# Runtime offsets loaded eight at a time, three cuts moved between engines, and the router product turned round, in a fused cross-attention and mixture-of-experts kernel

## What is computed

```python
x = x + tanh(g_xattn) * xattn(layernorm(x), ctx, mask, W, b)   # scores from relu projections, softmax over 77 keys
h = layernorm(x)
logits = h @ w_router                     # 8 experts, top 2, softmax over the two
moe = sum over the 2 chosen e of score * (silu(h @ fc1[e][:, :256]) * (h @ fc1[e][:, 256:])) @ fc2[e]
shared = (silu(h @ gate_w) * (h @ up_w)) @ down_w              # hidden width 512
x = x + tanh(g_ffn) * (moe + shared)
```

## Time and profile before

| | us |
|---|---|
| median of 3 runs | 240.33 |
| the profiled execution | 240.49 |
| its span in the trace | 238.8 |
| TensorE matmul busy | 216.5 (91%) |
| VectorE busy | 168.6 (71%) |
| ScalarE busy | 134.2 (56%) |
| GpSimd busy | 124.4 (52%) |

### The profile page before, as it was taken

How to read it: one execution, slowest core, us unless ns; L and a number is a source line. 1 busy time by engine, 2 the same in 40 slices (tenths; PEclk the granted TensorE clock), 3 DMA queues, 4 the chain that set the end, 5 groups by cost and what they waited for, 6 DMA issues and landing times.

```text
span 238.8 us, 5190 instructions
## 1 busy us (share of the span) xinstructions
PE 216.5 (91%) x1347; PEld 187.2 (78%) x1347; DVE 168.6 (71%) x513; ACT 134.2 (56%) x332; POOL 124.4 (52%) x178
## 2 busy tenths in 40 slices
PE   7988999999899999889727999999999999999982
PEld 7778899978687888668616788888888888887761
DVE  1978897797569799996912866666575666654893
ACT  2555888798769734445212465656566565655320
POOL 1698997554867877888400043434434343443600
PEclk9999999999999999999985999999999999999999
DMA  4999930000131225322003348475565646319787
GB/s 155 287 403 405 406 148 0 0 3 23 45 117 45 91 72 204 137 85 97 2 22 60 69 111 124 111 129 111 124 122 113 135 100 133 60 38 299 236 283 281
DMA packets 39347, 32.13 MB, mean 135 GB/s; under 512 B 29254, under 2 KB 30539, under 8 KB 39320
## 3 DMA queue, kind: packets, MB, share of 16 engines
q1 hardware_dynamic: 35312, 22.31, 34.0%
q0 software_dynamic: 3408, 8.53, 10.9%
q10 hardware_dynamic: 600, 0.97, 1.2%
HBM read 14.84 MB, written 12.75 MB: 116 GB/s over the span
## 4 chain that ended last, share of the span: by engine, by line
PE 59%; SPq 12%; issue 8%; DVE 8%; POOL 4%; DMA 3%; ACT 3%; DVEq 0%; POOLq 0%; ACTq 0%
PE bank L1028 41%; SPq L286 7%; PE bank L1291 3%; PE bank L1062 3%; PE bank L1074 2%; SPq L282 2%; DMA xt<-rows 2%; DMA acc<-in_x 2%; PE bank L1102 1%; PE bank L1164 1%; DVE act_lo L664 1%; SPq L281 1%; DVE acc L740 1%; PE bank L1112 1%; SPq L292 1%
## 5 line engine op out<-in xcount | busy, mean ns | idle before, releaser
L445 POOL DMA_INDIRECT parts<-y_out,dst x39 | 38.8, 995 | 70.9 <-DVE dst L957 46.1
L403 POOL DMA_INDIRECT rows<-hwords,slot x32 | 34.0, 1062 | 12.3 <-issue 10.7
L1028 PE MATMUL bank<-ew_hi,m_xt_hi 128*128 x78 | 31.6, 406 | 6.3 <-DVE m_xt_lo L664 6.3
L963 DVE TENSOR_TENSOR act<-act,bank 128x256 f32<-128x256 f32 x39 | 16.4, 421 | 29.5 <-issue 19.1
L615 ACT ACTIVATE act<-bank 128x256 f32<-128x256 f32 x39 | 15.0, 384 | 36.6 <-PE bank L1028 36.6
L1028 PE MATMUL bank<-ew_lo,m_xt_hi 128*128 x78 | 31.3, 401 | 0.0
L1028 PE MATMUL bank<-ew_hi,m_xt_lo 128*128 x78 | 31.3, 401 | 0.0
L1028 PE MATMUL bank<-ew_hi,act_hi 128*128 x78 | 25.2, 323 | 0.2 <-issue 0.2
L458 ACT ACTIVATE act_hi<-act 128x512 fp32r<-128x512 f32 x16 | 10.1, 629 | 25.4 <-DVE act L726 9.5
L664 DVE TENSOR_TENSOR m_xt_lo<-xt,m_xt_hi 128x256 fp32r<-128x256 f32 x39 | 16.2, 416 | 8.3 <-ACT m_xt_hi L458 8.3
L1028 PE MATMUL bank<-ew_lo,act_hi 128*128 x78 | 21.9, 280 | 0.0
(11 more groups left out here) (186 smaller groups left out, 644.4 us busy)
## 6 DMA issues: line engine op xcount, KB each, us to landing
ew_raw<-in_chunks SPq DMA_DIRECT2D x12, 512.0 KB, 10.7
low_buf<-parts SPq DMA_DIRECT2D x4, 512.0 KB, 3.6
high_buf<-parts SPq DMA_DIRECT2D x4, 512.0 KB, 4.0
acc<-in_x SPq DMA_DIRECT2D x7, 256.0 KB, 5.4
sw_raw<-in_chunks SPq DMA_DIRECT2D x3, 512.0 KB, 8.3
out<-acc SPq DMA_DIRECT2D x3, 512.0 KB, 3.3
rows<-pad_rows SPq DMA_DIRECT2D x9, 132.0 KB
xt<-rows SPq DMA_TRANSPOSE x39
```

The lines of the kernel that those rows point to most:

```text
L403: pool.indirect_dma_start(out=rows, out_offset=bass.IndirectOffsetOnAxis(ap=slot[:, h, k, i:i + 1], axis=0), in_=hwords[:, HT * h + i, :], ...
L445: pool.indirect_dma_start(out=parts, out_offset=bass.IndirectOffsetOnAxis(ap=dst[:, t:t + 1], axis=0), in_=y_out[:, t % SLOTS, :], in_offs ...
L963: TT(act[:, p, 0:I], act[:, p, 0:I], M_H[p][:, I:2 * I], ALU.mult).then_inc(s["m_prod"], 1)
L1028: ins = pe.matmul(ps, a, b, start=first and i == 0, stop=last and i == total - 1, skip_group_check=not lone)
```

## The change

Four edits.

1. SP reads the 39 offsets with five register loads of up to eight values, and without the bounds check behind each.
2. GpSimd's three `LAST` cuts go to VectorE, whose table gives units 7, 8, 10 and 11 one cut more and unit 12 one less. From unit 8 on, one cut stands ahead of `product_lo` and the rest behind it.
3. The router product is turned round. `wr` is widened to 352 columns a slice, zero but for 16, so that a window of 128 columns puts the 16 logits of group g on partitions 16 (g mod 4) and up. The weights stand still and 256 tokens move: four matmuls a group, four groups summed into the same 256 columns of bank 6. GpSimd clears `wr` at the start.
4. The logits of a half now lie with the experts on the partitions. VectorE copies them out (`cut_logits`), TensorE turns them back with two transposes (`turn_logits`) behind `gate(0)` and behind `gate(3)`, and VectorE reads them. In the last attention step VectorE's `turn_e` now stands ahead of `read_logits` and `first_choice`.

```diff
-LAST = tuple(range(CHUNKS - 3, CHUNKS))
-LATER = {3: 1, 4: 1, 5: 1, 6: 1, 7: 1, 8: 1, 9: 2, 10: 2, 11: 2, 12: 3}
+LATER = {3: 1, 4: 1, 5: 1, 6: 1, 7: 2, 8: 2, 9: 2, 10: 3, 11: 3, 12: 2}
...
-            off = [sp.value_load(t_off[0:1, t:t + 1], min_val=0, max_val=2 * PAD_ROW) for t in range(N_TILES)]
+            off = []
+            for t in range(0, N_TILES, 8):
+                off += nc.values_load_multi_w_load_instructions(
+                    t_off[0:1, t:min(t + 8, N_TILES)], engines=(mybir.EngineType.SP,), min_val=0, max_val=2 * PAD_ROW,
+                    skip_runtime_bounds_check_because="t_off is a row of the table or PAD_ROW, by construction")[1]
...
+            pool.memset(wr[:].bitcast(F32), 0.0).then_inc(s["wr_z"], 1)
...
-            for i in LAST:
-                cut_lo(pool, i)
...
+            def cut_logits(h):
+                after(v, "lg_ps", HG * (h + 1))
+                after(v, "lg_turned", h)
+                v.tensor_copy(lgt[:], bank[6][0:HG * 2 * E, 0:GN]).then_inc(s["lg_cut"], 1)
...
-                cut_later(u)
+                cut_later(u, slice(0, 1))
                 product_lo(u)
+                cut_later(u, slice(1, None))
...
             def router(g):
                 after(pe, "ht_l", g + 1)
+                at_ = g % HG
+                if at_ == 0:
+                    after(pe, "lg_cut", g // HG)
+                w_ = slice(WZ - 2 * E * at_, WZ - 2 * E * at_ + P)
+                for k in range(K):
+                    for x_ in (ht_hi, ht_lo):
+                        ins = pe.matmul(bank[6][:, 0:GN], wr[:, k, w_], x_[:, k, g * GN:(g + 1) * GN],
+                                        start=at_ == 0 and k == 0 and x_ is ht_hi,
+                                        stop=at_ == HG - 1 and k == K - 1 and x_ is ht_lo, skip_group_check=True)
+                ins.then_inc(s["lg_ps"], 1)
+
+            def turn_logits(h):
+                after(pe, "lg_cut", h + 1)
+                after(pe, "lg_read", h)
+                n_ = HG * 2 * E
                 for j in range(GT):
...
+                    ins = pe.transpose(bank[6][:, GN + j * n_:GN + (j + 1) * n_], lgt[:, j * P:(j + 1) * P],
+                                       ident[0:n_, 0:n_])
+                ins.then_inc(s["lg_turned"], 1)
...
             gate(0)
+            turn_logits(0)
             scores(NG - 1)
...
-            gate_up(3)
+            gate(3)
+            turn_logits(1)
+            up(3)
```

More of the change, by code:

```diff
@@ L47 @@
 HT = NT // NH
+HG = NG // NH
+WZ = 2 * E * (HG - 1)
 IN_A = 7
@@ L153, in build @@
         wr_raw = sm[:, 2 + K:].rearrange("p (k e) -> p k e", e=E)
-        wr = sb("wr", [P, K, 2 * E], F32R)
+        wr = sb("wr", [P, K, WZ + P], F32R)
+        lgt = sb("lgt", [HG * 2 * E, GN])
         tg = sb("tg", [P, 2])
@@ L207, in build @@
             xt_ps xt_h xt_l wt_h wt_l y_h y_l xp_ps xp sc_ps sc_in sc_max sc_exp eT_ps eT_h eT_l mt_ps s_inv resid stats2 mean2 pre2 pow2 rstd2 h_ready h_planes
-            hT_ps ht_h ht_l lg_ps lg_read rt picked rank_ps placed wts low_expert w_sign w_tanh fields slots t_expm scattered pads tb tiles_known
+            hT_ps ht_h ht_l wr_z lg_ps lg_cut lg_turned lg_read rt picked rank_ps placed wts low_expert w_sign w_tanh fields slots t_expm scattered pads tb tiles_known
             chunk_h chunk_lp chunk_lv gate_ps up_ps sil prod act_h act_l dn_ps dn_added
@@ L244, in by_pool @@
         def by_pool(i):
-            return i < IN_A or i in MID + LAST
+            return i < IN_A or i in MID
         def chunks_at(slot_):
@@ L469, in _ @@
             a.activation(tg[:], sm[:, 0:2], ACT.Tanh).then_inc(s["tanh_g"], 1)
-            hi(wr[:, :, 0:E], wr_raw, "wr_h")
+            after(a, "wr_z", 1)
+            hi(wr[:, :, WZ:WZ + E], wr_raw, "wr_h")
             a.wait_ge(wt_in, 16)
@@ L778, in then @@
                 v.wait_ge(s[name], n[name])
+            def cut_logits(h):
+                after(v, "lg_ps", HG * (h + 1))
+                after(v, "lg_turned", h)
+                v.tensor_copy(lgt[:], bank[6][0:HG * 2 * E, 0:GN]).then_inc(s["lg_cut"], 1)
             def read_logits(h):
-                after(v, "lg_ps", (NG // NH) * (h + 1))
-                lp = bank[6][:, HT * h * 2 * E:HT * (h + 1) * 2 * E].rearrange("p (t e) -> p t e", e=2 * E)
-                v.tensor_copy(lgx[:], lp).then_inc(s["lg_read"], 1)
+                after(v, "lg_turned", h + 1)
+                lp = bank[6][:, GN:GN + HT * 2 * E].rearrange("p (j g e) -> p g j e", j=GT, g=HG)
+                v.tensor_copy(lgx[:].rearrange("p (g j) e -> p g j e", j=GT), lp).then_inc(s["lg_read"], 1)
             def top(h, k):
@@ L822, in slots, with cut_later @@
                 v.tensor_copy(slot[:, h], slotf[:]).then_inc(s["slots"], 1)
-            def cut_later(u):
-                mine = [i for i in range(IN_A, CHUNKS) if i not in MID + LAST]
+            def cut_later(u, some=slice(None)):
+                mine = [i for i in range(IN_A, CHUNKS) if i not in MID]
                 first = sum(m for w, m in LATER.items() if w < u)
-                for i in mine[first:first + LATER.get(u, 0)]:
+                for i in mine[first:first + LATER.get(u, 0)][some]:
                     cut_lo(v, i)
@@ L884, in _ @@
             product_lo(2)
+            cut_logits(1)
             read_logits(1)
@@ L1107, in router @@
                 after(pe, "ht_l", g + 1)
-                for j in range(GT):
[L1109 to L1116, removed]
+                at_ = g % HG
[12 more added lines that the diff above has]
+                n_ = HG * 2 * E
+                for j in range(GT):
+                    ins = pe.transpose(bank[6][:, GN + j * n_:GN + (j + 1) * n_], lgt[:, j * P:(j + 1) * P],
+                                       ident[0:n_, 0:n_])
+                ins.then_inc(s["lg_turned"], 1)
             def rank_in_tile(h, ps):
@@ L1304, in _ @@
             down(U0 - 2)
-            after(pe, "chunk_lp", IN_A + len(MID + LAST))
-            after(pe, "chunk_lv", CHUNKS - IN_A - len(MID + LAST))
+            after(pe, "chunk_lp", IN_A + len(MID))
+            after(pe, "chunk_lv", CHUNKS - IN_A - len(MID))
             after(pe, "sil", U0)
```

7 lines of the change are left out of this document (4 added, 3 removed).

## The result

Four timed runs of the changed kernel gave 231.25 to 234.17 us, median 233.1; the kernel before had a median of 240.25 beside them (238.93 to 242.0). The ratio is 0.969, with a 95% interval from 0.960 to 0.978: faster. The forecast was 230.6 us with a range of 229.0 to 233.8. Direction and range held; of the 9.9 us that the sum promised, 7.2 came. The median lies outside the forecast's own range, 229.4 to 232, and inside that of rival B, 231.5 to 234, which had a chance of 0.15.

A forecast was written before the change was run, and what follows sets the result against it. SP's 39 offset reads were taken to delay the routed tiles. First load 8.9 us earlier plus 1.0 us from stage 1 makes 9.9 us off 240.49, so 230.6 us, range 229.0 to 233.8.

The forecast's parts named there:

- rival B: TensorE and VectorE arrive at the routed tiles later than the loads, through more stalls; 231.5 to 234 us, chance 0.15.
- the limit of 0.35 us a value: SP's offset loads: only above this price would they outlast their 10.6 us of slack and decide the first load.
- the old step of 0.57 us: SP's time per single offset read before, taken as the price of each wide load: five make about 3 us.
- the replay on the old scale: Stage 2's products and cuts from product 12 on, re-timed with edit 2: `m_up(0)` at 119.2 instead of 126.93 us.
- The stall of unit 8: TensorE's wait in stage 2, expected near 1.8 us after the change.
- I give them 0.6 us: Stage 1, VectorE's first and second choice ahead of the ranks: gain allowed despite an added copy of about 0.35 us.
- I take 1.0 us for stage 1 together: Edit 3's gain where unit 3 starts: 1.0 us earlier, between 0.4 and 3.0 us.
- GpSimd's later scatters ... so move too: Scatters from the cut at 72.17 us, which waits 1.48 us for ScalarE behind `gate(3)`, shift along with stage 1.
- The loads decide: Start of the routed tiles: first transposing load at 113.3 us sets the time; TensorE's path has 1.0 us to spare.
- Rival C: Router's saving reaches the scatters nearly whole, 2.0 to 3.0 us instead of 1.0; about 229 us, chance 0.08.
- D: Wide offset loads priced by value at the old step, so only stage 1's 1.0 us is kept; 239.5 us, chance 0.04.
- E: Wide offset loads cost more per value than the old step; at 0.8 us a value 248 us, chance 0.02.

The follow-up runs named there:

- e_offsets: The kernel before with edit 1 alone (five offset loads of eight, no bounds check); median 233.35 us, ratio 0.982 to before.
- a_no_router: The kernel before with edits 1 and 2, so without the turned router and its VectorE order; median 229.9 us, ratio 0.966 to before.
- k_fill: The changed kernel plus eight unused identity matmuls on TensorE ahead of the last attention step's `turn_e`; median 231.61 us, ratio 0.970 to before.
- l_singles: The changed kernel with 39 single offset loads instead of five of eight, still without bounds check; median 232.26 us, ratio 0.972 to before.
- f2: The changed kernel with GpSimd's cuts 5 and 6 moved between `weight_fields(0)` and the first scatter; median 230.75 us, ratio 0.966 to before.
- e_router: The kernel before with edits 3 and 4 alone (router turned round); median 241.55 us, ratio 1.014 to before.
- after_again: The changed kernel itself, unaltered, run again in a later set; median 231.63 us, ratio 0.963 to before.

## Why the prediction was right, and where its size was off

**Edit 1** was right. Five loads were taken at 3 us and cost 3.6; the limit of 0.35 us a value was not reached (about 0.09). What became late next was named rightly, the scattered rows. e_offsets has its first load at 114.36 us, where 114.3 was forecast. The Trainium skill's floor of about 600 ns for a `tensor_load` (DMA: Bandwidth & Descriptors, section Latency and other measured facts), quoted beside that term, is not borne out: single loads took 0.27 us and wide ones 0.52 to 0.94. Nor did the old step of 0.57 us speak for it, since the load was 0.27 us of that. The measurement decides; the sum did not rest on it.

**Edit 2** was right for TensorE: the idle time before `down(12)` is gone, and the replay on the old scale, `m_up(0)` at 119.2 us, is what a_no_router shows (119.23). The step that failed is that the first load was left at 114.3 us whatever edit 2 does. In a_no_router it came at 112.83, relative to x 1.7 us earlier than in e_offsets: the last scatter 1.2 us earlier, and its landing 0.5 us sooner. Since the loads did not decide in the end, this slip cost nothing. The stall of unit 8 was overrated, 1.40 us where "near 1.8" was forecast, and 1.14 in a_no_router.

**Edit 3** had the wrong sign, and that is where the time went. The failed step reads "I give them 0.6 us", for the choices, and "I take 1.0 us for stage 1 together". The local prices were sound: a router group took 0.55 us (forecast 0.48), steps 5 to 7 took 4.94 to 4.95 us each (forecast 4.9). But the sum took the choices at the length that they had before (they end at 51.85 us) and added a copy, although VectorE's and GpSimd's instructions beside each other had just been used to explain the 4.55 us of the earlier trace rows. The same rule (the Trainium skill, SBUF — State Buffer, section Who interferes with whom: two SBUF inputs on VectorE against a GpSimd instruction that reads SBUF, the later one waits for the whole of the other) bears on the choice, whose comparisons have two SBUF inputs; the rows of 1.19 and 1.21 us agree with it. Without the turned router one operation was hit so, 0.95 us long in a_no_router. The new order hits two, and both stand ahead of the softmax that TensorE waits for. At full clock the router's order and its way to the logits together cost 1.2 to 1.3 us at `m_up(0)` and at the last scatter (k_fill and l_singles against a_no_router), of which f2 gives back 0.7 to 0.9. In six of ten runs some 1.5 us of clock come on top. This is with edits 1 and 2 in; for the router alone e_router leaves it open.

**"GpSimd's later scatters ... so move too"** was the other half of the slip: they did move with stage 1, but to a later time.

**The end.** "The loads decide" with 1.0 us of slack for TensorE did not come out. In the changed kernel ScalarE cut the first two tiles at once behind the activation (no wait for a load), so TensorE's own stream decided, which is rival B, though for another reason than it gave: it expected more stalls in stage 2, and the time went at the end of stage 1. The loads decided in none of the runs with edit 1. Even in l_singles the chain that ended last goes from ScalarE's cut of the last activation over VectorE to `m_up(0)`, not over SP.

Put together from the traces, relative to x, at the start of `down(15)`: edits 1 and 2 gave 9.7 us (216.58 in a_no_router, 226.26 before) where 8.9 was forecast, and the router took 2.3 to 2.5 where it was to give 1.0. The final sums behind that were 0.9 to 1.1 us shorter than before, a gain that the forecast had left out ("nothing in the change touches them or the tail") and that no run explains. So the span gained 8.0 to 8.5 us against 9.9, a sum of one large miss and two smaller ones of the other sign; that the total came so near is luck, and so is a median inside the stated range, which it owes to the width given for rival B. By the timed runs, each set against its own before, a_no_router gained 8.5 us and the changed kernel 7.2 and 8.9. In the profiled execution x landed 0.55 us later than in that of before, hence its 7.5. Within stage 2 the forecast was close: from `gate(3)` to `m_up(0)` 51.8 us (before 58.5, forecast 50.8).

Rival C (stage 1 gives more) fell, D and E too: wide loads are not priced by value at the old step.

## What to carry to other kernels

When a change reorders one engine's short operations, lay the other engines' long ones over the new order, above all where a wait has just been explained by such an overlap; a stage's saved microseconds are worth only what the shared resource leaves. Moving the culprit is not the fix by itself: see first what stands behind it in its new place (here `rstd_second`), and what waits for that. And split a forecast of several edits into runs of one edit each: errors of opposite sign gave a sum that looked nearly right.

## What the runs showed of the hardware

- A register load of one value on SP takes 0.27 us and, one behind the other, 0.32 us; with its bounds check 0.57; one of eight values 0.52 to 0.94 us.
- Two 0.22 us VectorE operations with two SBUF inputs lasted 1.19 and 1.21 us beside two GpSimd cuts of 1.29 us. Three cuts on VectorE beside three on GpSimd took 5.86 us, which is the 2.1 us that they need alone and the 3.77 us of GpSimd's three, and those were no longer than elsewhere: VectorE bore the whole of it.
- It is not only operations with two SBUF inputs: beside a GpSimd cut of 1.34 us, a VectorE cast of 128x16 elements with one input lasted 0.83 us instead of 0.17 (f2_cuts_ahead).
- After TensorE idle times of 1.78 and 0.50 us with 0.8 us of work in 52 to 54 us, the granted clock was 0.58 in 54 to 56 and 0.57 in 56 to 58 us (the changed kernel); l_singles, with 1.76 and 0.50, and e_router, with 1.78 and 0.50, kept 1.00. The same idle time can cost about 1.3 us (last scatter of after_again against k_fill and l_singles) or nothing.
